# A new order for all steps of a two-layer transformer kernel, and three waits for buffers of its second layer

## The reference

```
q = (x @ Wq)  # 512 -> 32 heads x 128
k = (x @ Wk); v = (x @ Wv)  # 512 -> 8 heads x 128, each used by 4 query heads
probs = softmax(where(causal, q @ k.T / sqrt(128), -inf))
x = layernorm(x + (probs @ v) @ Wo)
w = sparsemax(x @ W_router.T + b_router)  # 8 experts
x = layernorm(x + x @ W_base.T + b_base + sum_e w[e] * (x @ A[e]) @ B[e])
```

## Time and profile before

| | us |
|---|---|
| three runs | 674.70, 674.86, 675.76 (median 674.86) |
| span of the profiled execution, first to last instruction | 673.6 |
| TensorE busy in it | 657.9 |
| VectorE, ScalarE, GpSimd busy | 531.2, 416.8, 259.1 |
| mean granted TensorE clock | 0.999 |

### The profile page before, as it was taken

One profiled execution on the slowest core, in us unless ns is written; L12 is line 12 of the kernel. 1 busy time (PEld: TensorE's weight loads), 2 busy tenths in 40 slices (PEclk: granted clock), 3 DMA queues, 4 the chain that ended last, 5 costly groups with the idle time before them and its releaser, 6 DMA issues.

```text
span 673.6 us, 11403 instructions
## 1 busy us (share of the span) xinstructions
PE 657.9 (98%) x3605; PEld 340.6 (51%) x3605; DVE 531.2 (79%) x1728; ACT 416.8 (62%) x1081; POOL 259.1 (38%) x246
## 2 busy tenths in 40 slices
PE   7899999999999999999999999999999999999996
PEld 3455455455555555455555545455554545455553
DVE  3899778867897688867797688867788578789866
ACT  3796665666556765667566765667556667866331
POOL 1686870166013750166013650167003613352231
PEclk9999999999999999999999999999999999999999
DMA  9357375354914285244924285353835247252602
GB/s 300 139 125 158 74 176 110 65 78 84 239 37 94 49 187 110 54 89 78 231 52 93 48 177 114 49 101 69 201 54 100 49 79 173 56 103 46 111 18 93
DMA packets 200779, 71.80 MB, mean 107 GB/s; under 512 B 169744, under 2 KB 192784, under 8 KB 200720
## 3 DMA queue, kind: packets, MB, share of 16 engines
q1 hardware_dynamic: 199376, 70.04, 48.4%
q10 hardware_dynamic: 1344, 1.05, 0.6%
HBM read 27.02 MB, written 2.10 MB: 43 GB/s over the span
## 4 chain that ended last, share of the span: by engine, by line
PE 89%; DVE 5%; DMA 3%; ACT 1%; POOL 1%; issue 1%; SPq 0%; DVEq 0%; POOLq 0%
PE bank L1259 23%; PE bank L1210 21%; PE bank L1249 15%; PE bank L1234 12%; PE bank L1222 5%; PE bank L1190 4%; PE bank L1291 2%; PE bank L1203 2%; PE bank L1193 2%; DMA pT<-p 2%; DVE p L1065 1%; PE bank L1183 1%; DVE pr L1045 1%; DVE rowmax L946 1%; PE bank L1302 1%
## 5 line engine op out<-in xcount | busy, mean ns | idle before, releaser
L741 POOL TENSOR_SCALAR raw<-raw,scale_of 128x512 f32<-128x512 f32 (+1 forms) x75 | 120.6, 1608 | 315.3 <-ACT wk L807 189.1
L1045 DVE CUSTOM_DVE_ANT_0 pr<-bank,mask,back_of 128x32 f32<-128x32 f32 (+15 forms) x256 | 125.3, 496 | 58.4 <-PE bank L1234 57.6
L863 ACT ACTIVATE pr<-pr,mx 128x288 f32<-128x288 f32 (+15 forms) x256 | 131.0, 512 | 61.2 <-DVE mx L1045 60.3
L1210 PE MATMUL bank<-xT,wq 128*128 128x512 f16 x720 | 164.5, 379 | 0.3 <-DVE y L1082 0.3
L872 ACT ACTIVATE p<-pr,ri 128x32 f16<-128x32 f32 (+15 forms) x256 | 118.4, 511 | 49.7 <-DVE ri L1056 49.5
L1065 DVE SCALAR_TENSOR_TENSOR p<-pr,ri,p 128x448 f16<-128x448 f32 (+15 forms) x256 | 128.4, 545 | 15.9 <-ACT p L872 14.7
L1234 PE MATMUL bank<-kT,qT 128*128 128x32 f16 (+15 forms) x768 | 122.2, 279 | 3.9 <-DVE qT L925 2.4
L1249 PE MATMUL bank<-pT,v 128*128 128x512 f16 x480 | 122.8, 379 | 0.8 <-DMA pT<-p 0.7
L1210 PEld LDWEIGHTS bank<-xT,wq 128*128 128x128 f16 x720 | 70.2, 98 | 82.1 <-DVE y L1082 0.8
L1234 PEld LDWEIGHTS bank<-kT,qT 128*128 128x128 f16 x768 | 67.7, 98 | 62.4 <-issue 3.9
L1259 PE MATMUL bank<-wo_odd,oT 128*128 128x512 f16 x384 | 96.1, 379 | 0.0
(11 more groups left out here) (145 smaller groups left out, 692.3 us busy)
## 6 DMA issues: line engine op xcount, KB each, us to landing
raw<-in_wo SPq DMA_DIRECT2D x32, 256.0 KB, 3.5
raw<-in_wq SPq DMA_DIRECT2D x30, 256.0 KB, 3.9
raw<-in_wk SPq DMA_DIRECT2D x8, 256.0 KB, 4.3
raw<-in_wv SPq DMA_DIRECT2D x8, 256.0 KB, 4.1
y<-in_x SPq DMA_DIRECT2D x1, 2048.0 KB, 13.0
pT<-p SPq DMA_TRANSPOSE x128, 3.7
out<-y SPq DMA_DIRECT2D x8, 256.0 KB, 2.0
...
```

Of the source, the lines that this page charges most:

```text
L741: eng.tensor_scalar(whole, raw_of(name, key), scale[0], None, ALU.mult).then_inc(sems["scaled"], 1)
L863: eng.activation(pr[:, t % 2, h, 0:w], pr[:, t % 2, h, 0:w], ACT.Exp, bias=mx[:, k:k + 1], scale=-1.0, accum_out=rs[:, k:k + 1]).then_inc( ...
L1045: eng.tensor_tensor_reduce(out=pr[:, t % 2, h, 0:w], in0=psum("S", t, h)[:, 0:w], in1=mask[:, 0:w], scale=score_scale(t), scalar=BIG, op0= ...
L1210: made = eng.matmul(out, wq[:, g % 2, w, h, c * 128:(c + 1) * 128], xT[:, x, c, b * 512:(b + 1) * 512], start=c == 0 and w + x == 0, stop= ...
```

## The change

All three step tables are replaced. Each new table holds the same steps as the old one, each once, in another order; FIRST (the steps that read unsplit float32 pieces), the split of work between engines and every instruction stay. Three waits are added: `sp(k)` on ScalarE waits until hw(k-2) is made before it writes rl, VectorE waits for the transpose ht(k-2) before it writes hw(k), and for nmr(k-4) before it writes the second statistics.

```diff
@@ FIRST_STEPS @@
     ("fetch", "x", 1, 1), ("fetch", "x", 1, 2), ("fetch", "x", 1, 3), ("fetch", "wo", 0, 0), ("fetch", "wo", 0, 1), ("fetch", "wo", 0, 2),
-    ("fetch", "wo", 0, 3), ("consts",), ("most", "k", 0), ("table",), ("most", "x", 0, 0), ("most", "q", 0), ("most", "x", 0, 2), ("rows",),
-    ("most", "x", 0, 1), ("bits", "A"), ("K", 0), ("turn", "A"), ("bits", "B"), ("factor", "A"), ("Q", 0, 0), ("turn", "B"), ("factor", "B"),
-    ("x", 0, 1), ("most", "v", 0), ("most", "x", 1), ("bits", "C"), ("Q", 0, 1), ("x", 0, 2), ("K_lo", 0), ("x", 0, 0), ("Q", 0, 3), ("turn", "C"),
-    ("x", 0, 3), ("Q", 0, 2), ("wv", 0, 0), ("factor", "C"), ("S", 0, 0), ("S", 0, 1), ("wv", 0, 1), ("exp", 0, 1), ("Q_lo", 0, 2), ("S", 0, 2),
-    ("S", 0, 3), ("S", 1, 0), ("wq", 0, 0), ("S", 1, 1), ("exp", 0, 0), ("most", "o", 0), ("inv", 0, 0), ("exp", 0, 3), ("exp", 1, 1), ("x", 1, 3),
...
+    ("fetch", "wo", 0, 3), ("consts",), ("most", "k", 0), ("most", "q", 0), ("K", 0), ("turn", "A"), ("x", 0, 3), ("most", "x", 0, 0), ("x", 0, 2),
+    ("most", "x", 0, 1), ("most", "x", 1), ("most", "x", 0, 2), ("Q", 0, 0), ("fetch", "wq", 1, 1), ("bits", "A"), ("factor", "A"), ("wq", 0, 0),
+    ("most", "v", 0), ("bits", "B"), ("turn", "B"), ("Q", 0, 1), ("turn", "C"), ("K_lo", 0), ("factor", "B"), ("bits", "C"), ("most", "o", 0),
+    ("factor", "C"), ("wk", 0), ("x", 0, 1), ("wv", 0, 0), ("wv", 0, 1), ("x", 1, 1), ("wq", 0, 1), ("x", 0, 0), ("Q", 0, 2), ("Q", 0, 3),
+    ("Vp", 0, 3), ("x", 1, 0), ("S", 0, 1), ("S", 0, 2), ("S", 0, 0), ("fetch", "wk", 1), ("bits", "D"), ("exp", 0, 1), ("Vp", 0, 0), ("S", 0, 3),
+    ("Q_lo", 0, 0), ("S", 1, 0), ("x", 1, 3), ("exp", 0, 0), ("x", 1, 2), ("S", 1, 2), ("Vp", 0, 2), ("exp", 0, 2), ("Q_lo", 0, 2), ("wq", 0, 2),
+    ("fetch", "wq", 1, 3), ("turn", "D"), ("S", 1, 1), ("fetch", "wq", 1, 2), ("inv", 0, 1), ("inv", 0, 0), ("fetch", "wv", 1, 0), ("Vp", 0, 1),
+    ("S", 1, 3), ("exp", 0, 3), ("exp", 1, 2), ("norm", 0, 1), ("exp", 1, 1), ("norm", 0, 0), ("Q", 1, 0), ("factor", "D"), ("rest", 0, 1),
+    ("most", "k", 1), ("fetch", "wv", 1, 1), ("rest", 0, 0), ("exp", 1, 0), ("wq", 0, 3), ("fetch", "wq", 1, 0), ("exp", 1, 3), ("wo", 0, 3),
+    ("S", 2, 2), ("S", 2, 0), ("inv", 1, 1), ("inv", 1, 0), ("wo", 0, 0), ("S", 2, 1), ("rows",), ("Vp", 0, 5), ("Vp", 0, 4), ("norm", 1, 1),
+    ("rest", 1, 1), ("exp", 2, 2), ("S", 2, 3), ("exp", 2, 0), ("fetch", "wo", 1, 1), ("rest", 1, 0), ("norm", 1, 0), ("exp", 2, 3), ("wo", 0, 1),
...
@@ LAST_STEPS @@
-    ("F", 4), ("ht", 6), ("base", 7, 0, 3), ("sp", 7), ("F", 5), ("st2", 5), ("ht", 7), ("F", 6), ("base", 7, 3, 4), ("F", 7), ("st2", 6),
-    ("fin", 4), ("fin", 5), ("st2", 7), ("fin", 6), ("fin", 7),
...
+    ("ln1", 7), ("ht", 4), ("F", 3), ("ht", 5), ("R", 6), ("zt", 7), ("sp", 6), ("F", 4), ("base", 6, 0, 4), ("ht", 6), ("fin", 3), ("R", 7),
+    ("F", 5), ("base", 7, 0, 3), ("sp", 7), ("st2", 5), ("ht", 7), ("fin", 4), ("F", 6), ("st2", 6), ("fin", 5), ("base", 7, 3, 4), ("st2", 7),
+    ("F", 7), ("fin", 6), ("fin", 7),
@@ ScalarE, step sp @@
                     act.wait_ge(*done("R", k))
+                    if k > 1:
+                        act.wait_ge(*done("hw", k - 2))
@@ VectorE, step sp @@
                     dve.wait_ge(*done("sp4", k))
+                    if k > 1:
+                        dve.wait_ge(*done("ht", k - 2))
@@ VectorE, step st2 @@
                     dve.wait_ge(*done("F", k))
+                    if k > 3:
+                        dve.wait_ge(*done("nmr", k - 4))
```

More of the change, by code:

```diff
@@ L131 @@
+    ("rest", 1, 1), ("exp", 2, 2), ("S", 2, 3), ("exp", 2, 0), ("fetch", "wo", 1, 1), ("rest", 1, 0), ("norm", 1, 0), ("exp", 2, 3), ("wo", 0, 1),
+    ("inv", 2, 1), ("Q", 1, 1), ("norm", 2, 1), ("S", 3, 0), ("rest", 2, 1), ("exp", 2, 1), ("inv", 2, 0), ("most", "q", 1), ("Q", 1, 2), ("S", 3, 1),
+    ("exp", 3, 0), ("norm", 2, 0), ("rest", 2, 0), ("exp", 3, 1), ("S", 3, 2), ("wo", 0, 2), ("K", 1), ("Q_lo", 0, 3), ("PV", 0, 0), ("table",),
[10 rows of a table added]
 )
 NEXT_STEPS = (
-    ("S", 6, 0), ("fetch", "wo", 2, 1), ("fetch", "wq", 2, 3), ("Q", 2, 1), ("fetch", "wo", 2, 0), ("fetch", "wq", 2, 1), ("S", 6, 1), ("PV", 4, 0),
@@ L158 @@
[L158 to L159 removed]
[10 rows of a table removed]
[L170 removed]
[8 rows of a table removed]
[L179 removed]
+    ("Q", 2, 2), ("fetch", "wq", 2, 1), ("S", 6, 1), ("S", 6, 2), ("Q", 2, 3), ("S", 6, 0), ("W", 3, 0), ("fetch", "wo", 2, 0), ("S", 6, 3),
@@ new lines @@
+    ("norm", 12, 0), ("S", 13, 3), ("exp", 13, 2), ("exp", 14, 0), ("S", 14, 0), ("PV", 10, 1), ("W", 9, 2), ("inv", 13, 1), ("exp", 13, 3),
[8 rows of a table added]
+    ("S", 17, 1), ("exp", 16, 3), ("inv", 16, 1), ("exp", 16, 2), ("Q", 5, 0), ("W", 12, 1), ("exp", 17, 2), ("exp", 16, 1), ("PV", 14, 1),
+    ("W", 12, 2), ("bits", ("ov", 3)), ("norm", 16, 1), ("inv", 16, 0), ("W", 12, 3), ("S", 17, 0), ("PV", 14, 2), ("PV", 15, 0), ("Vp", 1, 4),
+    ("exp", 17, 0), ("rest", 16, 1), ("exp", 17, 1), ("rest", 16, 0), ("norm", 16, 0), ("S", 17, 3), ("S", 18, 2), ("PV", 15, 1), ("PV", 15, 2),
@@ new lines @@
+    ("Q", 5, 1), ("S", 18, 0), ("inv", 17, 1), ("W", 13, 3), ("exp", 17, 3), ("Vp", 1, 5), ("turn", ("qk", 3)), ("inv", 17, 0), ("PV", 15, 3),
+    ("factor", ("qk", 3)), ("S", 18, 1), ("S", 18, 3), ("exp", 18, 3), ("norm", 17, 1), ("wq", 3, 0), ("rest", 17, 0), ("W", 14, 0), ("norm", 17, 0),
+    ("turn", ("ov", 3)), ("exp", 18, 0), ("exp", 18, 1), ("rest", 17, 1), ("exp", 18, 2), ("factor", ("ov", 3)), ("inv", 18, 1), ("W", 14, 1),
+    ("S", 19, 1), ("W", 14, 2), ("inv", 18, 0), ("K", 5), ("W", 15, 0), ("W", 15, 1), ("S", 19, 0), ("inv", 19, 0), ("norm", 18, 1), ("exp", 19, 1),
@@ L180 @@
+    ("norm", 21, 0), ("rest", 21, 0), ("PV", 19, 3), ("wv", 2, 1), ("K", 6),
 )
 LAST_STEPS = (
[L182 to L184 removed]
[4 rows of a table removed]
@@ L189 @@
-    ("one", 2), ("S", 57, 1), ("exp", 56, 2), ("W", 54, 0), ("fetch", "wb", 3), ("exp", 56, 3), ("S", 57, 2), ("inv", 56, 1), ("norm", 56, 1),
-    ("rest", 56, 1), ("W", 54, 1), ("W", 54, 2), ("inv", 56, 0), ("exp", 57, 0), ("exp", 57, 2), ("W", 54, 3), ("one", 1), ("PV", 55, 0), ("one", 0),
-    ("norm", 56, 0), ("rest", 56, 0), ("PV", 55, 1), ("exp", 57, 1), ("PV", 55, 2), ("S", 57, 3), ("inv", 57, 0), ("one", 3), ("most", "r", 0),
-    ("S", 58, 0), ("PV", 55, 3), ("S", 58, 1), ("exp", 57, 3), ("most", "b", 0), ("S", 58, 2), ("inv", 57, 1), ("norm", 57, 1), ("S", 58, 3),
@@ L193 @@
-    ("bits", "ffn"), ("Q", 15, 0), ("W", 55, 0), ("exp", 58, 2), ("turn", "ffn"), ("rest", 57, 1), ("norm", 57, 0), ("factor", "ffn"),
-    ("exp", 58, 1), ("rest", 57, 0), ("exp", 58, 3), ("S", 59, 0), ("S", 59, 1), ("exp", 58, 0), ("S", 59, 2), ("inv", 58, 1), ("lb",), ("Q", 15, 3),
-    ("inv", 58, 0), ("norm", 58, 0), ("rest", 58, 0), ("K", 15), ("exp", 59, 1), ("W", 55, 1), ("exp", 59, 0), ("PV", 56, 0), ("PV", 57, 0),
-    ("wra",), ("exp", 59, 2), ("inv", 59, 0), ("norm", 58, 1), ("W", 55, 2), ("W", 55, 3), ("S", 59, 3), ("norm", 59, 0), ("rest", 58, 1), ("bias",),
@@ L207 @@
-    ("rest", 62, 0), ("norm", 62, 1), ("PV", 61, 0), ("PV", 61, 1), ("zt", 1), ("rest", 62, 1), ("W", 60, 1), ("S", 63, 3), ("st1", 3), ("F", 0),
-    ("ln1", 3), ("W", 60, 2), ("exp", 63, 2), ("exp", 63, 3), ("R", 1), ("inv", 63, 1), ("W", 60, 3), ("norm", 63, 0), ("base", 1, 0, 4),
[7 rows of a table removed]
-    ("fin", 4), ("fin", 5), ("st2", 7), ("fin", 6), ("fin", 7),
+    ("exp", 54, 2), ("S", 54, 1), ("S", 54, 0), ("S", 54, 2), ("wo", 7, 2), ("Q", 14, 2), ("W", 51, 0), ("fetch", "wb", 2), ("one", 2),
+    ("exp", 54, 1), ("S", 54, 3), ("fetch", "wb", 1), ("exp", 54, 0), ("fetch", "wra"), ("norm", 54, 0), ("S", 55, 1), ("S", 55, 2), ("exp", 54, 3),
@@ new lines @@
+    ("most", "r", 0), ("one", 1), ("fetch", "wb", 3), ("fetch", "lb"), ("norm", 54, 1), ("inv", 54, 0), ("exp", 55, 1), ("exp", 55, 0), ("S", 55, 0),
[3 rows of a table added]
+    ("S", 56, 0), ("PV", 54, 0), ("S", 56, 3), ("exp", 56, 0), ("most", "l", 0), ("inv", 55, 1), ("one", 0), ("rest", 55, 0), ("exp", 56, 1),
+    ("exp", 56, 3), ("rest", 55, 1), ("S", 57, 1), ("norm", 56, 1), ("W", 53, 1), ("S", 57, 2), ("S", 57, 0), ("K", 15), ("inv", 56, 1),
+    ("exp", 57, 2), ("W", 52, 2), ("bits", "ffn"), ("rest", 56, 1), ("S", 57, 3), ("PV", 54, 1), ("inv", 56, 0), ("S", 58, 2), ("rest", 56, 0),
@@ new lines @@
+    ("PV", 54, 2), ("S", 58, 0), ("norm", 56, 0), ("W", 52, 3), ("Q", 15, 0), ("W", 53, 2), ("inv", 57, 0), ("S", 58, 1), ("turn", "ffn"),
+    ("inv", 57, 1), ("exp", 57, 0), ("factor", "ffn"), ("exp", 57, 1), ("PV", 55, 0), ("S", 58, 3), ("rest", 57, 1), ("exp", 57, 3), ("norm", 57, 1),
+    ("exp", 58, 2), ("exp", 58, 1), ("exp", 58, 0), ("exp", 58, 3), ("W", 54, 0), ("norm", 57, 0), ("rest", 57, 0), ("PV", 55, 1), ("PV", 55, 2),
+    ("S", 59, 1), ("inv", 58, 0), ("inv", 58, 1), ("W", 54, 1), ("rest", 58, 1), ("wra",), ("PV", 55, 3), ("norm", 58, 1), ("norm", 58, 0),
[11 rows of a table added]
@@ L217 @@
```

(4 more changed lines are left out.)

47 lines of the change are left out of this document (16 added, 31 removed), and 105 rows, old and new, of tables (FIRST_STEPS, LAST_STEPS, NEXT_STEPS).

## The result

The changed kernel takes 688.18 us (median of 4 runs, 686.99 to 688.48), the kernel before 674.97 us beside it: a ratio of 1.0193, 95% interval [1.0179, 1.0207]. It is slower by 13.2 us. The forecast was 671.7 us, with a range up to 676.0: wrong in size and in sign.

A forecast was written before the change was run, and what follows sets the result against it. TensorE was taken as the bound, busy 657.9 of 673.6 us, leaving 15.7 us idle. Terms -0.2 - 2.2 + 0 - 0.25 - 0.5 = -3.15 took 674.86 to 671.7 us, range 669.8 to 676.0.

The forecast's parts named there:

- Part 1: Up to the first scores: first S at 28.1 to 28.3 us, idle 1.3 to 1.5 against 1.66; -0.2 us.
- Part 2: From 27 to 60 us: waits for maxima and q go, 2.7 us of waits fall to 0.5; -2.2 us.
- lag count: VectorE's queued work against TensorE's at each S, from the first: lag 9.7 us at S(3,2) before, 4.3 at most after.
- Part 3: Loading rows later: y lands about 50 us, rest(1)'s transposes 53.7, before PV(1,0) at 54.4; 0 us, bounds 0 and +6.8.
- rival A: At PV(1,0), y delays the transposes: a wait of 6.8 us, 678.5 us in all; chance 0.10.
- y's own share is 5.3 us: In the move of rows: y's load time without queueing, from br's 8.2 and y's 13.0 us landings, issued 0.5 us apart.
- Part 4: Repeated block and single waits: 0.7 us of waits in all for 1.0 before; -0.25 us, bounds -1.0 and +3.
- rival B: Repeated block: eight short Q to S distances and three passes over 1.0 us banks cost +2.4, 674.1 us; chance 0.18.
- stays hidden: Repeated block: GpSimd's 2.8 us a piece is covered, as weights have 7.5 us or more from step to use.
- Part 5: The tail: last W to the span's end takes 24.0 us against 24.8; -0.5 us, bounds -1.0 and +0.7.
- TensorE's 657.9 us stay: Whole kernel: no operation is added or taken away, so TensorE's busy time is unchanged and only its 15.7 us idle can change.
- C: First scores come late: factor C behind the wo maximum, plus the table load, +1.5, 673.2 us; chance 0.15.

The follow-up runs named there:

- table_front: The changed kernel with the step table back at the front, behind the maximum over wk: 687.23 us (1.0172).
- rows_front: The changed kernel with rows (bb, br and y's 2 MB) moved back to its old place at the front: 680.93 us (1.0082).
- only_waits: The kernel before with only the three added waits, all steps in the old order: 674.76 us (1.0000).

## Why the prediction was wrong, by its own steps

**Part 1, the first scores: -0.2 foretold, +1.3 of idle measured.** The first S stands at 29.64, not 28.1 to 28.3. The link that was mis-sized is VectorE's low halves. They were priced at 0.65 to 0.75 from q's, which have only one input in SBUF; those of wv and of one x piece have two and took 1.65 and 1.17 us beside GpSimd. Without these losses of 1.3 us the q low halves would end at 28.2, where 28.0 was foretold. GpSimd itself was walked for the weights' due times but not for the first Vp, which waited for it (2.07 us). The table load, given 0.3 us "inside the bounds", did delay the first square sum from 10.96 to 12.26, and this profile has 1.01 us of waiting for stage B; but moving it back left the first S where it was (table_front), so it alone is not what made the scores late.

**Part 2, 27 to 60 us: -2.2 foretold, right.** The waits of 2.7 us are down to 0.65, none of them for a maximum or for q. The lag count of VectorE against TensorE did what it was used for.

**Part 3, rows: 0 foretold, a wait of 4.24 us measured, near 6 us with its clock.** (rows_front gave back 7.25, some 1.7 of it clock behind another pause.) This step alone loses the sign, and rival A, given 0.10, was the one that came true: at the named place, PV(1,0), with 4.24 us inside its bound of 6.8. The step that failed is "y's own share is 5.3 us", taken from the distance of two landings: y took 11.4 us from issue to landing, close to the only figure measured whole (13.0). rows was also issued at 47.1, not 43.1 to 44.5. And a wait of this length has a second price that no part of the sum had: the products behind it run at the lower clock.

**Part 4, the repeated list and the last one: -0.25 foretold, +6.65 measured.** The kind of mishap was rival B's, its place and size were not. The eight short distances from Q to S, the reason for B, never bit. What bit was a bank 1.3 us late at S(14,2) in each pass and oT low halves in the last list. Sums of engine times by queue cannot show it: VectorE's queue had the room, but stood still for an exp at its head, and its rests have no fixed price beside GpSimd. The statement that GpSimd "stays hidden" looked only at when its results are due, not at what it does to VectorE while it runs. The added waits cost nothing that can be told, as foretold (only_waits).

**Part 5, the tail: -0.5 foretold, about right.** Read as the prediction read it, from the last W to the end of the span, 24.6 us became 23.9, where 24.8 to 24.0 was foretold. The idle time behind the last product fell by only 0.1 us; the rest is product time behind the last W, 18.8 us for 19.4. The last list alone costs 1.9 us, so nothing of the gain is left.

In idle time of TensorE the parts came out 1.5 (part 1), 0 (part 2), 4.2 (part 3), 6.9 (part 4) and 0.4 us (part 5) worse than foretold, and the clock, in no part, adds 2.9: 15.9 of the 16.0 us from the sum made on the span (673.6 - 3.15 = 670.45) to 686.5. Part 3 or part 4 alone lost the sign. The sentence "TensorE's 657.9 us stay" failed too: they became 660.8. The chances (0.13 for slower) treated A, B and C as rare single mishaps beside a known path. Measured, a mishap of the kind of each happened, all in one kernel. The lower end of the range does not come out of its own terms either: parts 2 and 5 at their ends give 670.7 us, not 669.8.
